# Order of the denominator and output matmuls in an attention loop: d, o, d, o becomes d, d, o, o

## The reference

```python
q = jnp.einsum('bse,hed->bhsd', x, Wq) + bq[None, :, None, :]
kg = jnp.einsum('bse,ged->bgsd', x, Wk) + bk[None, :, None, :]
vg = jnp.einsum('bse,ged->bgsd', x, Wv) + bv[None, :, None, :]
k = jnp.repeat(kg, per, axis=1)
v = jnp.repeat(vg, per, axis=1)
scores = jnp.einsum('bhqd,bhkd->bhqk', q, k) * (1.0 / np.sqrt(d))
scores = jnp.where(causal[None, None, :, :], -jnp.inf, scores)
attn = jax.nn.softmax(scores, axis=-1)
out = jnp.einsum('bhqk,bhkd->bhqd', attn, v)
...
x = _layernorm(x + attention(x))
x = _layernorm(x + ffn(x))
# ffn: h = fwht(x*SU_ug)/S; h = silu(h@Wg.T*..) * (h@Wu.T*..); y = (fwht(h*SU_dp)/S)@Wd.T*..
```

## Time and profile before

| | us |
|---|---|
| median of 2 runs | 3466.11 |
| these runs | 3416.56 and 3515.65 |
| profiled execution, its own time | 3180.44 |
| its span, slowest core (core 3) | 3179.4 |
| spans of all eight cores | 3158.4 to 3179.4 |
| granted TensorE clock, mean, by core | 0.916 to 0.921 |

### The profile page before, as it was taken

The page is one execution under the profiler, slowest core; times in us unless marked ns, Lnnn a source line. Parts: engine busy times, 40 slices in busy tenths (PEclk is TensorE's granted clock), DMA queues, the critical chain, the costliest instruction groups (busy, mean ns, idle before and its releaser), DMA issues.

```text
span 3179.4 us, 28896 instructions; the slowest of 8 cores (3158.4 to 3179.4 us)
## 1 busy us (share of the span) xinstructions
PE 2665.2 (84%) x11068; PEld 1042.5 (33%) x11068; DVE 590.7 (19%) x629; ACT 638.5 (20%) x616; POOL 121.9 (4%) x211
## 2 busy tenths in 40 slices
PE   3999992999999999842199999999999649999970
PEld 1444441222222222210044444444444214444430
DVE  0222220111111111253211111111111230000014
ACT  0000000665655656531000000000000120000010
POOL 1000000000000000000000000000000000000000
PEclk9999996999999989965599999999999879999985
DMA  9348647002001000001734444444444483554426
GB/s 153 72 77 137 111 88 185 13 1 40 1 21 20 1 0 1 1 17 46 185 78 92 96 87 99 87 95 94 89 97 87 117 186 80 119 106 103 110 67 198
DMA packets 109027, 258.74 MB, mean 81 GB/s; under 512 B 22624, under 2 KB 63584, under 8 KB 103776
## 3 DMA queue, kind: packets, MB, share of 16 engines
q0 software_dynamic: 56112, 155.83, 28.8%
q1 hardware_dynamic: 51832, 95.84, 9.6%
q10 hardware_dynamic: 952, 5.24, 0.7%
HBM read 337.19 MB, written 58.72 MB: 125 GB/s over the span
## 4 chain that ended last, share of the span: by engine, by line
PE 80%; DMA 9%; DVE 4%; ACT 3%; issue 2%; another core or an unknown queue 1%; POOL 0%; DVEq 0%; SPq 0%; ACTq 0%; POOLq 0%
PE ps_ug_a L164 15%; PE ps_y L164 14%; PE ps_ug_b L164 14%; PE ps_ring L164 14%; PE ps_o L407 7%; PE ps_d L403 7%; PE ps_s L164 6%; DMA AR<-scr_f 2%; DMA ARF<-scr_f 2%; DMA ARF<-xkvA 2%; DMA out<-stg_f 1%; ACT stg_b L460 1%; PE ps_rd L376 1%; DMA ARF<-xq 1%
## 5 line engine op out<-in xcount | busy, mean ns | idle before, releaser
L164 PE MATMUL ps_s<-QSB,AR 128*128 128x512 bf16 x768 | 241.8, 399 | 90.1 <-DMA AR<-scr_vt 56.2
L164 PE MATMUL ps_ug_a<-AR,QSB 128*128 128x512 bf16 x1344 | 296.9, 379 | 0.0
L164 PE MATMUL ps_ug_b<-AR,QSB 128*128 128x512 bf16 x1344 | 296.9, 379 | 0.0
L768 ACT ACTIVATE stg_b<-ps_ug_b,sgate 128x1024 bf16<-128x1024 f32 x64 | 71.3, 1114 | 826.0 <-PE ps_ug_b L164 826.0
L164 PE MATMUL ps_y<-ARF,QSB 128*128 128x512 bf16 x1024 | 225.4, 381 | 4.2 <-issue 4.2
L164 PE MATMUL ps_ring<-ARF,AR 128*128 128x512 bf16 x768 | 169.7, 382 | 53.9 <-DMA ARF<-xkvA 53.9
L164 PEld LDWEIGHTS ps_ug_b<-AR,QSB 128*128 128x128 bf16 x1344 | 131.5, 98 | 158.6
L164 PEld LDWEIGHTS ps_ug_a<-AR,QSB 128*128 128x128 bf16 x1344 | 131.5, 98 | 158.6
L164 PE MATMUL ps_y<-AR,QSB 128*128 128x512 bf16 x832 | 182.2, 379 | 0.0
L403 PE MATMUL ps_d<-AR,ones_b 128*1 128x512 bf16 x384 | 150.8, 393 | 20.6 <-DVE rowbuf L421 20.6
L164 PE MATMUL ps_ring<-AR,ARF 128*128 128x512 bf16 x768 | 167.7, 379 | 0.0
(11 more groups left out here) (120 smaller groups left out, 1853.1 us busy)
## 6 DMA issues: line engine op xcount, KB each, us to landing
QSB<-WdownT POOLq DMA_DIRECT2D x16, 2048.0 KB, 16.2
QSB<-WupT POOLq DMA_DIRECT2D x42, 512.0 KB, 5.5
QSB<-WgateT POOLq DMA_DIRECT2D x42, 512.0 KB, 7.4
ARF<-xkvB POOLq DMA_DIRECT2D x8, 2048.0 KB, 20.1
scr_f<-QSB SPq DMA_DIRECT2D x64, 256.0 KB, 2.0
WBUF<-WupT POOLq DMA_DIRECT2D x22, 512.0 KB, 5.5
WBUF<-WgateT POOLq DMA_DIRECT2D x22, 512.0 KB, 7.5
ARF<-xkvA POOLq DMA_DIRECT2D x4, 2048.0 KB, 40.7
```

Of the source, the lines that this page charges most:

```text
L164: return pe_.matmul(out_ap, lhsT, rhs, start=start, stop=stop, skip_group_check=True)
L768: acv = p.inc(ac_.activation(gsl_ring[pb], pg[:, :], AF.Silu, bias=0.0, scale=sgate[:, c:c + 1]), "ac")
```

## The change

In `emit_dav` the loop over `k2` is split in two. The two denominator matmuls are emitted first, then the two output matmuls. Their operands, their `start` and `stop` flags, the waits ahead of them and the semaphore increment on the last matmul stay as they are. `kt` is worked out again in the second loop.

```diff
                                ebuf[eb][:, k2 * 512:(k2 + 1) * 512],
                                start=(kt == 0), stop=(kt == npair * 2 - 1),
                                skip_group_check=True)
+                for k2 in range(2):
+                    kt = pr * 2 + k2
                     inst = pe_.matmul(
                         ps_o[ob],
                         vslot[s][:, (vtbase + kt) * 128:(vtbase + kt + 1) * 128],
```

## The result

| | before | after |
|---|---|---|
| median | 3276.15 us (10 runs, 3173.77 to 3515.65) | 3307.35 us (11 runs, 3110.77 to 3468.14) |
| ratio after / before (runs at the normal clock) | | 0.9793, 95% interval 0.9776 to 0.981 |
| lowest run | 3173.77 us | 3110.77 us |
| profiled execution, its span | 3180.44, 3179.4 us | 3118.53, 3117.5 us |
| attention stage, mean of the 8 cores | 785.8 us | 719.2 us |

In some executions of any of these kernels the cores of one die, or of both, show a lower granted clock and the time is 3 to 15% longer (in one of the kernel after, cores 0 to 3 took 3097 to 3107 us at a clock of 0.917 to 0.919 and cores 4 to 7 took 3376 to 3393 us at 0.822 to 0.831); the medians mix both kinds, so the ratio, which leaves such runs out, is the measurement here, and the medians say nothing of the change. The kernel became 2.1% faster (1.9 to 2.2%).

What follows compares the result with a forecast made beforehand. TensorE's own matmul sequence was taken to bound the attention stage. 77.6 us saved, less 5.7 at stripe ends and 3 for the ScalarE loop, gave 69 us: 3180.4 to 3111, ratio 0.978, scaled to 3390 us, range 3200 to 3460.

Steps and rivals of the forecast that it cites:

- The step that read rows 4: Four adjacent denominator matmuls in another stage start 0.213 us apart, so only switching stationary width is dear, about 0.31 us.
- The rival by which only half is gained: In attention pairs, output matmul after output matmul stays dear; 38 us saved, 3142 us, or 3424 on the median; chance 0.08.
- the one by which nothing changes: Exposed time belongs to each denominator and output matmul, not the switch; gain 0, 3180 us, median 3466; chance 0.05.
- the rule of the Trainium skill that spoke against the change: Attention matmuls share all 128 rows, so weight loads behind equal shapes stay exposed too; saving 0 us.
- The sum: Attention stage saving: 77.6 - 5.7 - 3 = 69 us, from 3180.4 to 3111 us, a ratio of 0.978.
- Step 1: Saving per emit_dav call: two fewer width switches, 0.202 us on each of 384 pairs, 77.6 us in all.
- Step 2: At stripe ends PE waits for DVE and ACT, so 28 pairs gain nothing; 5.7 us taken off.
- Step 3: ScalarE loop of 1.50 us per pair meets PE's 1.49; costs 0.01 on some 320 pairs, 3 us.
- the rival of more drops: Longer idle at stripe ends brings more half-clock stretches; slower, 3239 us, or 3530 on the median; chance 0.05.
- the forecast of 3111: Whole kernel at the profiled execution's level: 3180.4 us less the 69 us saved in attention.
- I scale: 3466.11 x 0.978 = 3390: Whole kernel: median of the runs shown, 9% above the profiled execution, times the forecast ratio, giving the point 3390 us.

Runs made afterwards that it cites:

- the runs with and without the loop: The changed kernel as it is (rerun: ratio 0.979), and with pairs delayed by three instead of four (two lowest runs 3100.32 and 3101.4 us, giving 0.974).
- o, o, d, d: The changed kernel with each pair's two output matmuls emitted before its two denominator matmuls; ratio 0.9747 (0.9721 to 0.9772).

## Why the prediction was right or wrong

**What the change does: right.** The step that read rows 4, that a d behind a d is as cheap as any matmul, came out as 215 ns. d to o stayed at 310, s to d at 307. The rival by which only half is gained, and the one by which nothing changes, had the distances to show in the first place and fell at them. For the rule of the Trainium skill that spoke against the change ("TensorE: Matmul & The Clock Gate", "The mechanism": a load overlaps matmuls in flight only when the row group differs), the trace of after disagrees once more: all operands have the same 128 rows, and the loads behind an equal shape are hidden at 215 ns. The same section has a second case that the prediction left out, a load into the background weight buffer; the traces agree with that one as far as equal widths go.

**The size: right to a few microseconds, on the stage.** The sum said 69 us. Measured, as the mean of the eight cores, it is 66.6; without clock drops 63.2. Three terms were off, each by a little.
- Step 1 took o to o as 0.215 from the s-s spacing; it is 0.226. But those 11 ns only moved. The matmul behind the first full-width one after a switch comes 11 ns late: before, that was the second d (o to d 320, s to d 309) and the next s (227), now it is the second o, and the s behind it is back at 216 where no loop holds it. Without the loop a pair is 1.493 us, 0.197 less than 1.690, where 0.202 was forecast. 384 x 0.005 = 1.9 us.
- Step 2 said that the saving turns into wait at the ends of stripes, and took off 5.7 us; the waits of the scores there grew by 6.8, so 1.1 us more.
- Step 3 gave the ScalarE loop 0.01 us a pair, 3 us; the runs with and without the loop put it at 5.8, so 2.8 us more.

69 - 1.9 - 1.1 - 2.8 = 63.2. That this meets the 63.2 of the stage to the tenth is chance, since the clock drops are taken off by an estimate that is good to some 3 us. The clock went the other way, 67.6 to 61.0 us at half level, 1 to 3 us gained; the rival of more drops fell. On the profiled level the forecast of 3111 stands against timed runs from 3110.77 to 3112.52 us, and the ratio of 0.978 against 0.9793. The profiled executions alone give less, 3180.44 to 3118.53, 62 us.

**The time: wrong by its scale.** The step that failed is "I scale: 3466.11 x 0.978 = 3390". The median of the two runs shown was taken for a level of the kernel that the change shortens by its ratio. What the runs show in its place is two groups for each kernel. Before: four runs from 3173.77 to 3179.23 us and six from 3274.93 to 3515.65. After: four from 3110.77 to 3112.52 and seven from 3298.33 to 3468.14. The change moved the lower group by 67 us, and the upper one is not the lower one times a constant: in the run of 3393.83 us four cores took 3097 to 3107 us, as in the lower group, and the rest came with the lower clock of the other four. Both medians fall into the upper group, at its low end, and so they went the other way than forecast, up from 3276.15 to 3307.35 us, while the kernel became faster.

The measured median lies 83 us under the point and inside the range of 3200 to 3460. That is the merit of a wide range, not of the mechanism: the median of before lies in it too. The profiled level, 3111, would have been no better a point for the median, 196 us under it. What the profile allowed to forecast is the ratio and the lower group; of the median only that it lies somewhere between the two groups' ends. The spread of 3% between the two runs shown, and their 7 and 11% above a profiled execution whose cores all agreed within 1% and at one clock, was in the table, and I read it as a level.

Two readings in the prediction are loose, and nothing hangs on them: of the first ten entries of the chain seven are PE's and three are DMAs, and 3103 to 3120 us scaled to the median is 3382 to 3400, not 3375 to 3405.

**The chances.** 0.51 for faster by over 2% and 0.46 for within 2% fit a result of 2.07% whose interval, 1.9 to 2.2%, leaves open on which side of 2% it lies.

## What to carry to other kernels

When matmuls with narrow stationary operands (up to 64 columns) are mixed with full ones, count the switches per iteration, and take the cost from differences of starts, not from busy times. Grouping equal widths halves the switches. Padding the narrow operand to 65 columns or more removes them all and costs nothing in PE time here; padded to 128 it can replace a broadcast as well. And before shortening one engine's part of a loop, work out the next limit: here the loop through ScalarE lay so close behind that it already cost 0.015 us a pair, and it had to be loosened (one pair less of delay, worth 0.15% in the kernel before) for a larger gain to be paid out.

## What the runs showed of the hardware

- From 128 columns to 1 or 64 and from 1 to 128 the hand-over costs about 95 ns beyond the 215 of a 512-column matmul (309); with 65, 127 and 128 it costs nothing measurable. In a steady pair the load under such a hand-over starts with its own matmul (901.77 and 902.09 above), or 0.01 us before it. The Trainium skill, "TensorEngine Tiling (Array Packing)", "Tiling Modes", lists 128x128, 128x64 and 128x32 as ways to divide the array, and says that changing the mode drains the engine; the border between 64 and 65 columns agrees with it. That a matmul with few stationary columns counts as such a mode is my reading, and no run here shows the drain itself. Widths of 32 and below, apart from 1, weren't tried.
- From 64 columns to 128 the hand-over is dearer (336 ns) than from 1 column (309). Why is open.
- With 128 columns of ones, the hand-over from o to the broadcast matmul (1 row x 128 columns, float32) still takes 309 ns. It differs from its neighbours in rows and in type, and no run parts the two.
- The matmul after the first full-width one behind a switch starts 11 ns late: 226 to 227 ns for 215 (o to s before, o to o after, s to s with o, o, d, d), and 320 for 309 (o to d before). Why is open.
- Half-clock stretches, mostly of 3.4 us, some of 10.2 at the ends of groups, followed some of the idle spots of about 1 us at stripes' ends and not others, and their sum changed from 67.6 to 41.2 us with changes of 0.2 us or less in a pair's length. Between the kernel before and the changed one with pairs delayed by three they make 10 to 13 us of the stage, more than the ScalarE loop's 5.8. Each sum is of one profiled execution; only the changed kernel was profiled twice (61.0 and 60.1 us).
